# Eleven-block layer stack on one core: scan side work redistributed over VectorE, ScalarE and GpSimd, with new issue orders

## The reference

```python
xc = conv_general_dilated(xi, conv_w, ...)       # 4 taps, depthwise, along time
xi = silu(xc + conv_b)
dt, Bm, Cm = split(xi @ x_proj.T, ...)
dt = softplus(dt @ dt_w.T + dt_b)
dA = exp(dt[..., None] * A);  dBx = (dt * xi)[..., None] * Bm
h  = dA * h + dBx                                 # the recurrence over 512 tokens
y  = sum_over_states(h * C) + xi * D
y  = (y * silu(z)) @ out_proj.T
```

## Time and profile before

| | us |
|---|---|
| median of 3 runs | 3326.03 (3322.09 to 3331.97) |
| profiled execution: its own time | 3321.42 |
| profiled execution: span, first to last instruction | 3319.6 |
| busy PE / DVE / ACT / POOL | 2674.8 / 2515.0 / 1659.4 / 1577.2 |

### The profile page before, as it was taken

How to read it: one execution, slowest core, us unless ns; L and a number is a source line. 1 busy time by engine, 2 the same in 40 slices (tenths; PEclk the granted TensorE clock), 3 DMA queues, 4 the chain that set the end, 5 groups by cost and what they waited for, 6 DMA issues and landing times.

```text
span 3319.6 us, 30398 instructions
## 1 busy us (share of the span) xinstructions
PE 2674.8 (81%) x8498; PEld 889.4 (27%) x8498; DVE 2515.0 (76%) x3637; ACT 1659.4 (50%) x2752; POOL 1577.2 (48%) x1301
## 2 busy tenths in 40 slices
PE   5676757979698988998689976997579877998887
PEld 1222212323122322233222321232122322232222
DVE  1588988787988889788977798878988887246351
...
GB/s 82 55 102 83 96 107 44 78 101 68 93 46 82 76 126 51 90 68 99 109 40 97 69 119 52 72 80 95 106 53 103 77 118 17 45 53 80 43 31 42
DMA packets 160088, 253.13 MB, mean 76 GB/s; under 512 B 20144, under 2 KB 57904, under 8 KB 159664
## 3 DMA queue, kind: packets, MB, share of 16 engines
...
## 4 chain that ended last, share of the span: by engine, by line
PE 50%; DVE 28%; ACT 10%; issue 8%; POOL 3%; DMA 1%; DVEq 0%; SPq 0%; POOLq 0%; ACTq 0%
PE ps L507 50%; DVE rh L1257 7%; DVE nmx L1179 5%; DVE xib L1243 2%; DVE rh L1263 2%; ACT ps L1557 2%; ACT tN L1503 1%; ACT L1304 1%; DVE xif L1243 1%; DVE tF L1121 1%; POOL tF L1632 1%; POOL rb L1612 1%; DVE tF L1126 1%; DVE tL L1168 1%; ACT ps L1317 1%
## 5 line engine op out<-in xcount | busy, mean ns | idle before, releaser
L1257 DVE TENSOR_TENSOR_SCAN rh<-ps,rb 128x512 f32<-128x512 f32 x512 | 622.9, 1217 | 117.0 <-ACT ps L1557 103.4
L1179 DVE TENSOR_REDUCE nmx<-ps 128x1 f32<-128x512 f32 (+3 forms) x864 | 529.9, 661 | 84.9 <-PE ps L507 82.9
L1503 ACT ACTIVATE tN<-ps 128x512 f32<-128x512 f32 (+1 forms) x896 | 460.9, 564 | 230.4 <-PE ps L507 228.2
L1602 POOL TENSOR_TENSOR rh<-rh,cs 128x512 f32<-128x512 f32 x208 | 308.6, 1487 | 437.4 <-DVE rh L1257 437.1
L507 PE MATMUL ps<-tN,strip 128*64 128x512 f32 (+3 forms) x2048 | 484.4, 564 | 12.0 <-DVE hN L1201 9.2
L1612 POOL TENSOR_TENSOR rb<-duf,bs 128x512 f32<-128x512 f32 x256 | 369.1, 1456 | 227.2 <-DVE rh L1257 225.9
L507 PE MATMUL ps<-hF,W 128*128 128x512 f32 x592 | 361.7, 696 | 59.8 <-DVE tF L1121 37.5
L1612 POOL TENSOR_TENSOR rb<-dub,bs 128x512 f32<-128x512 f32 x256 | 369.0, 1459 | 65.9 <-DVE rh L1257 63.1
L507 PE MATMUL ps<-Ks,Qs 48*128 48x512 bf16 (+3 forms) x1024 | 325.8, 409 | 83.8 <-DVE nmx L1179 82.1
L1626 POOL TENSOR_TENSOR tF<-tF,cr 128x512 f32<-128x512 f32 x128 | 172.0, 1345 | 363.8 <-DVE tF L1126 253.0
L507 PE MATMUL ps<-tF,W 128*128 128x512 f32 x544 | 306.7, 656 | 39.7 <-POOL tF L1632 30.9
...
## 6 DMA issues: line engine op xcount, KB each, us to landing
cr<-shares SPq DMA_DIRECT2D x256, 256.0 KB, 3.3
bs<-rowsf SPq DMA_DIRECT2D x128, 256.0 KB, 3.6
cs<-rowsf SPq DMA_DIRECT2D x128, 256.0 KB, 3.2
bs<-rowsb SPq DMA_DIRECT2D x128, 256.0 KB, 3.6
cs<-rowsb SPq DMA_DIRECT2D x128, 256.0 KB, 3.4
...
```

What stands on the lines that cost most here:

```text
L1179: red(nmx[:, 4 * qt + 2 * (i // 4) + a, i % 4:i % 4 + k], o[:, 0:k * nk].rearrange("p (k c) -> p k c", k=k), AX.X, ALU.max, negate=True).t ...
L1257: eng.tensor_tensor_scan(rh[n % NH][:, g, :], PS, rb[n % NBB][:, g, :], 0.0, ALU.mult, ALU.add).then_inc(s_h, 1)
L1503: act(tN[m % NP][:, a, 0:nq], PA[a][:, 0:nq], ACT.Exp).then_inc(s_ex, 1)
L1602: tt(h, h, cs[n % NB][:, :], ALU.mult).then_inc(s_cp, 1)
```

## The change

- The first tap and its bias (32 instructions of 128×512) go from DVE to ACT, as an Identity activation with scale and bias. The wait for the scaled weights of batch 0 goes with it.
- The positive parts (32) go from DVE to ACT, as Relu with a bias. They now stand between |v| and its exp on ACT.
- The products with D (32) go from DVE to ACT, as Copy with a scale, behind the wait for POOL's dt·xi. What waited for DVE's `yi1` now waits for ACT's.
- In the 208 later steps DVE multiplies by C in every fourth step, in place of every second: 52 DVE products of 128×1024 go, and 104 POOL products of 128×512 come.
- DVE's scaling of the weights for M (`setup_later`) is now a step of its own in DVE's list.
- Every string of `ORDER` is new. ACT's list has 138 table loads by the built program, where the list before has 150 (one of these stands ahead of the first activation).

```diff
@@ ORDER: all strings are replaced, as this line of "sp" @@
-        "M1S21M1S43M1S29F1S2F5S1M1F1S5F1S1F1S13P2S2P2S2P1S3P1S6M1S7X1S12F6S4F2S2F1S6M1S4P5F1P1F3S4F3S2F2X1S2F4S2F1S2F4S"
+        "M1S19M1S45M1S32F5M1F1S3F1S2F1S2F1S12P1S2P3S2P1S2P1S7M1S7X1S18F1S1F3S1F1S2F2S2F1S1F1M1S9P5F1P1F3S6F3S2F2X1S2F4S"
...
@@ KINDS @@
-    "pre": chain("in0 in1 xp dt0 dt1", "si0 si1 pj ab0 ex0 ln0 ab1 ex1 ln1",
-                 "c00 c10 c20 c30 xs0 c01 c11 c21 c31 xs1 mx0 dt0 mx1 dt1 yi0 yi1", "du", ln={}),
+    "pre": chain("in0 in1 xp dt0 dt1", "c00 si0 c01 si1 pj ab0 mx0 ex0 ln0 ab1 mx1 ex1 ln1 yi0 yi1",
+                 "c10 c20 c30 xs0 c11 c21 c31 xs1 dt0 dt1", "du", ln={}),
@@ who multiplies by C @@
-            return n < EARLY or n % 2 == 1
+            return n < EARLY or n % 4 == 1
@@ vector_engine, pre @@
-                if j.b == 0:
-                    eng.wait_ge(s_set, SET["mw"])
...
-                    eng.wait_ge(*j.pe(f"in{g}"))
-                    ts(c, PM, cw[:, 4 * g + 3:4 * g + 4], w(f"m{p}_cb", g, g + 1), ALU.mult, ALU.add).then_inc(
-                        *M.by_dve(j, f"c0{g}"))
-                    yield
...
-                        eng.wait_ge(*j.dve(f"c{d - 1}{g}"))
+                        eng.wait_ge(*(j.dve(f"c{d - 1}{g}") if d > 1 else j.act(f"c0{g}")))
...
-                    eng.wait_ge(*j.act(f"ab{g}"))
-                    ts(dt[p][:, g, :], PM, w(f"m{p}_db", g, g + 1), 0.0, ALU.add, ALU.max).then_inc(
-                        *M.by_dve(j, f"mx{g}"))
-                    yield
                     eng.wait_ge(*j.act(f"ln{g}"))
-                    eng.wait_ge(*j.dve(f"mx{g}"))
                     tt(dt[p][:, g, :], dt[p][:, g, :], PM, ALU.add).then_inc(*M.by_dve(j, f"dt{g}"))
-                    yield
-                eng.wait_ge(*j.pool("du"))
-                for g in range(2):
-                    ts(xi[p][:, g, :], xi[p][:, g, :], w(f"m{p}_dd", g, g + 1), None, ALU.mult).then_inc(
-                        *M.by_dve(j, f"yi{g}"))
@@ scalar_engine, pre @@
+                    if (j.b, g) == (0, 0):
+                        eng.wait_ge(s_set, SET["mw"])
+                    eng.wait_ge(*j.pe(f"in{g}"))
+                    act(du[p][:, g, :], PM, ACT.Identity, bias=w(f"m{p}_cb", g, g + 1),
+                        scale=w(f"m{p}_cw", 4 * g + 3, 4 * g + 4)).then_inc(*M.by_act(j, f"c0{g}"))
+                    yield
...
+                    act(dt[p][:, g, :], PM, ACT.Relu, bias=w(f"m{p}_db", g, g + 1)).then_inc(*M.by_act(j, f"mx{g}"))
+                    yield
...
-                    eng.wait_ge(*j.dve(f"mx{g}"))
+                    eng.wait_ge(*j.act(f"mx{g}"))
                     act(PM, a, ACT.Ln, bias=one).then_inc(*M.by_act(j, f"ln{g}"))
+                    yield
+                eng.wait_ge(*j.pool("du"))
+                for g in range(2):
+                    act(xi[p][:, g, :], xi[p][:, g, :], ACT.Copy, scale=w(f"m{p}_dd", g, g + 1)).then_inc(
+                        *M.by_act(j, f"yi{g}"))
                     yield
```

More of the change, by code:

```diff
@@ L61 @@
+        "S2P2S2P2S4F9S2X1S4F4S2F1S1F4S9P4S2P1S2P1S4F1S2F3M1S2F1S2F1S4F3S1F1S3X1S6F4S2F2S2F1S2F1M1S2F1S10P5F1P1F3S5F3S1F"
+        "2X1F1S2F3S2F5S10P2S2P2S2P1S2F1P1F3S2F1S3M1S1F1S2F3S3F1S5F5X1F1S2F1S2F2S6M1S8P4S4F4P1F1P1F1S2F3S2X1F4S2F5S12P4S"
+        "4P1S2P1S2F1S2F3S3F6X1F9P4F6P2F7X1F5P1F1P1F3P2F5P1F1P1F9X1F9P6X1F20"
     ),
     "pe": (
[L63 to L64 removed]
@@ new lines @@
+        "1M1F2S1F1M1F2M1F9L8M1L1X2L1X4L1X3L1X2L2X1L2M1X1L1M1X1L1M2X4M1X2M1X3L1X2L1X4M1L1X5L1X3L1X5M1X2L1X1M1L1A1L2M1A1M"
+        "1A1M1L1A4F1A2F1A2M1A1F2A5F1A5F1A3F2A4F2A19F3A1F4M1F9M1F2M1F6M1F3L1F1L1F1M1L1F2L1M1L1F1L1F2L1F1M1F2L1F1L1F1X2L1"
+        "X14F2X3L1F2X3L1F1X2F2X3L1X1F1X2F2X1F1X2L1F2X3F1X2F2X3F2X3F1L1F1X1L1F1A1M1F1A4M1A2F1A2F1A2M1A4F1A1F1A1F1A2F2A1F"
+        "1A2F1A1F1A2L1M1L1A1L1A2L1A3L1A2L1A2L1A10L1A3L1A1M1X2L1M1L1X3L1X2M1X4L1X4L1X4M1X3L1X7M1X7M1X3L1M1X5M1X1L1X1L1X8"
+        "F1X3F1X3M1X2F2X2F1X1F1L1F1A1F1A4F2A32F1A2F2A2M1F1A2F2A3F1A2F2A1F1A2F2A2F1A2F2A2F1A2F2A2F1A2F2A1M1F1M1F2A2M1F3L"
@@ new lines @@
+        "1F1M1L1F1L2F1L1F2L1F2L1F1M1F2L1F1X2F1X2L1X2M1X1L1X8F2X3F2X3L1F1X3F2X3F1X1L1F2X3F1X2F2X3L1F1X3L1F2X3F2X2F1L1F1X"
+        "1L1F1M1A1F1M1A6F1A2F1A2M1A6F1A1F1A2F1A1F2A2F1A2M1F2L1F1L1A2L1A2F1L1A2L1A2L1A2F1A2M1A2M1A9L1F2L1M1L1A1L1F1X2L1M"
+        "1X1F1M1X2L1X2F1X4M1F2M1F2M1F1X3L1X2L1X6F1X3F1X3M1X2L1F2X4F1X2F1X3L1F1X3F1X4F2X2L2F1X3F2X3F1X2F2X1F1X3F2X1F1X3L"
+        "1F3X1F3A1F2A2F1A2F2A2F1A2F2A2F2A2M1F1A2L1A2F1L1A2F1A4M1A2M1A8L1A2L1A2L1A2F2A8L1A4L1A2M1A4L1A4L1A2X1A1X4A1F1X2L"
+        "1F2X3L1F1X3F3X3L1F2X3F1X1M1X1F2X3L1X1F1X2F2X3F1X2F2X2F1X3L1F2X3F1X2F2X2F2L1F1X1L1F1A1F1A6M1A2F1A8F1A2F1A6F4A1F"
@@ new lines @@
+        "1A1F1A2F2A2L1A2F1L1A2F1L1A2L1A2F1L1A2L1A2L1A4M1A1L2M2F1X2F1M1X1M1X2M1F1M1F1X1A1X1F1X1M1X5F2X4M1F1X1F1M1F1X11M1"
+        "X3L1X2M1X1L1M1X3L1X5F1X3F1X3M1X1L1F2X3L1X1F1X2F1X2F1X3F1L1X3F3L1F2X1L2F3A1F1L1F2A2F1A2M1F2A4F1A2F2A2F1A2F2A2M1"
+        "F1A2M1F2A2F1A2F2A2F2A3F1A3L1A2F1L1M1F1A1L1A1L1A2L1A2F2A12L1A4L1A6L1A2M1X1A1X2L1X2A1F1X2F2X3L1F1X3F2X3F1X2F2X3F"
+        "1X2F2X3F1X1F2X1L1F1X3L1F2X3F1X2F2L1X3F1X1L1F4X3L1X1F2X1L1F1A2F1A7M1A4F1A2F1A4M1A1F1A2F1A1F2A2M1F3M1F1L1F1L1A2F"
+        "1M1L1A2L1A2F1L1A2L1A2L1A8L1A4L1A1X2M1X2F2M1X2M1A1X2F1M1X3L1X2F1L2X3M1F2X2F1M1F1X3F1X1F1X2L1X2L1X8M1X3L1X7M1X4M"
@@ L167 @@
+        "1S4F1S2M1S1F2S1F1S1F3L1S4M1S5L1S1A1S5A1S1A1S6F2S1A1S1F1S2F1A1S4F1S3F1A1S2F1S2F1S13A2S5M1S1F2S1L1F1S3F5S1A1S4A1"
+        "F3A1F3S1F2S4A1S7A1S5A1S3A1S1M1S1A1S12F1S9F3S1F1S1F1M1S2F2S3M1S7F1S1F1S3F1S2F1S3F1A1S3F1S2A1F1S1F1S3A1S5A1S9A1S"
+        "3A1S5A1S2F2A1S1F6S2M1S2A1S1F3S1F3S1F2A2S6A1S10A1S3A1S4A1S4A1S5M1S14F1S2F2S1F1S1F2S1F1S1F1M1F3A1F2A1F2A1F1A4F3A"
+        "1F13A4F3A1F1A1F4A2F8A1F3A1F5A7F1A1F5A1F2A3F8"
     ),
@@ L399, in build @@
         for b in range(B):
-            pre_f, pre_b = ([jm[b, n].pool("du"), jm[b, n].dve("yi1"), (s_rows[p], 16 * (b + 1))] for n, p in
+            pre_f, pre_b = ([jm[b, n].pool("du"), jm[b, n].act("yi1"), (s_rows[p], 16 * (b + 1))] for n, p in
                             (("mf", "f"), ("mb", "b")))
```

191 lines of the change are left out of this document (85 added, 106 removed).

## The result

| | before | after |
|---|---|---|
| median, us (4 runs each on the same chip) | 3326.2 | 3297.2 (3295.98 to 3302.93) |
| ratio, with 95% interval | 1 | 0.9915 (0.9896 to 0.9934) |
| profiled execution: own time / span, us | 3321.42 / 3319.6 | 3298.37 / 3296.5 |

The kernel became faster by 0.85%, some 28 us. The forecast was 3260, a change of −62 us on the profiled execution; the sign was right and less than half of the size came. 3297 lies in the range of 3190 to 3335 and next to the time of rival C (3300).

A forecast was written before the change was run, and what follows sets the result against it. DVE was taken to lead the first two busy stages, close to PE in the middle, PE the tail. From 3321.4: −94 + 10 + 15 + 7 = −62, so 3259, 3264 as median, stated as 3260 us; 8-in-10 range 3190 to 3335.

The forecast's parts named there:

- rival C: PE takes over at once: only DVE's chain share, 58 us, counts against 32 us of costs; −26, 3300; chance 0.20.
- The order, priced at 0 ± 25: All engines' rewoven lists: the same strands overlap in the same way, so 0 us, ±25.
- The weight of 0.6: DVE: 0.6 of the 157 us that leave it counts as gain, 94 us, with bounds 58 and 157.
- its lower bound: DVE's relief counted only by its share of the chain, 28 of 76 points, 37%: 58 us gained.
- the count of 20-us windows: Middle stage: 116 windows sorted by DVE's busy time, counting in full, half or not; 0.55, taken as 0.6.
- The costs of 32 us: On POOL, SBUF and ACT: 10 for the queue, 15 for shared reading, 7 for later exponentials.
- The queue: On POOL: late products delay the next `rb`, then scans and DVE's adds; 10 us, bounds 0 and 57.
- the 7 forecast: On ACT: new work delays exponentials that DVE's scans wait for; 7 us, bounds 0 and 25.
- Shared reading: DVE's adds slowed by POOL's SBUF work: 15 us, bounds 0 and 110; mean add 1.5 to 1.6 us.
- Rival D's point, 1.88: Mean DVE add, in us, from which moved products blocking adds would decide; the rival has +33, 3359; chance 0.15.
- The tail "as long as now": Tail, 560 us, would keep its length; 20 us or more longer would be the order.
- The sign of the queue: DVE waiting for POOL's products or `rb` by more than 30 us in all would show the queue.

The follow-up runs named there:

- short_both_old: old_both with all moved work on POOL and ACT cut to 8 of 512 columns, those values left out; 0.9898 of the kernel before, 3292.58 us.
- old_both: Kernel before with its old lists and both moves (products by C to POOL, three kinds of operations to ACT); 1.0104, 3367.11 us.
- new_order: Kernel before with all strings of `ORDER` new and neither move; 1.0208, 3401.03 us.
- relief_old: Kernel before with the work taken from DVE cut to 8 of 512 columns (from batch 1 on), nothing put elsewhere; 0.9896, 3298.25 us.
- old_tail: Kernel after with the lists of before from a little behind the last scan on; 0.9872 of the kernel before, 3292.79 us.
- relief_two: relief_old plus the 256 expert up-projection matmuls on PE at 256 of 512 columns, those values left out; 0.9771 of the kernel before, 3254.30 us.

## Why the prediction was wrong in size

The table can be walked in two ways from before to after. In the old lists first: relief −34 us (short_both_old), price of the moved work +69 (old_both against it), new lists −63 (after against old_both: 1.0104 − 0.9915). Or in the new lists: the lists alone +69 (new_order), relief −108 (1.0208 − 0.9883), price +11. Both give −28. The prediction had −94, +32 and 0, in all −62.

- **The order, priced at 0 ± 25, is the step that failed by either walk**: −63 or +69, by what it is put on, and more than twice the bound. The prediction treated it as a remainder, since the same strands overlap in the same way; no row had priced it. The table shows that the worth of the moves and that of the lists can't be priced apart.
- **The weight of 0.6 failed in the lists from which it was read.** The 157 us that leave DVE were about right (155.8 by the rows; DVE's busy time fell by 102.5). That 0.6 of them, 94 us, would be gained was not: in the old lists all of them bring 34 us, and the first 97 bring 35, 0.36 each. The prediction had the right number for that beside it, 0.37 from the earlier trace rows, as its lower bound, and set it aside for the count of 20-us windows. A window in which DVE is busy 95% says that DVE is full there. It doesn't say that the other engines can run earlier by what it sheds; in relief_old the waits for exponentials (103.4 to 127.5 us) and PE's share of the chain (50 to 54) grew. In the new lists the weight was 0.66 to 0.71, so by that walk 0.6 was near. That is luck: no row of those lists was read for it.
- **The costs of 32 us were less than half of the price in the old lists** (69: POOL 48, ACT 21) and three times that in the new (11). The queue was looked for behind `rb`, while in old_both PE's wait for the expert products grew, 30.9 to 43.0 us; the prediction named these products and put no price on them. The wait for `rb` did go up in the middle stage, from 12.0 us to 25.5, for a queue priced at 10. But new_order has 28.5 us in all with no product moved, so it is in the main the lists' and not the products'. The wait for exponentials grew by 20 us in the stage for the 7 forecast. Part of that is no cost of the work on ACT: it grew by 24 us in relief_old, where ACT got nothing.
- **Shared reading** came as forecast in size: the mean add is 1.61 us (334.9 over 208), at the upper edge of 1.5 to 1.6, and the adds cost 21 us more in all for 15. Rival D's point, 1.88, was not reached. But new_order has 1.582 without a moved product, and old_both 1.600 in the old lists: lists and products each bring most of the rise alone, and the forecast had only the products. And the adds were not all that is held up: small SBUF work on DVE took more too, and so DVE's busy time is 2412.5 where 2373 was forecast.
- **The sum was helped by luck.** By the first walk it came within 37 us of the time only because two errors to one side (the gain too high by 60, the costs too low by 37) met an order better by 63; the rest is in rounding (its sum gives 3264, and it says 3260). By the second, the gain too low by 14 and the costs too high by 21 met an order worse by 69.
- **The tail "as long as now"** failed by 20 us. The sign was named ahead (20 us or more would be the order), and old_tail shows that it was.
- **Rival C** has the time, 3300, but not the mechanism. Of the 58 us that it grants the relief, the old lists paid 34; its costs of 32 were a middle between the two sets of lists; it had no term for the order either. Its sign, PE's waits for DVE unchanged, did not show (461 to 410 us), and relief_two shows that PE and DVE are both paid.
- **Right**: 100 products with 141.3 us (140); POOL 1721.6 (1735); ACT 1694.2 (1710). **Missed** beside what is named above: the middle stage is 31 us shorter and not 55 to 70; DVE's wait for exponentials in it is 107 us for 94. The sign of the queue, more than 30 us of waiting for `rb` in all, showed with 32.5; by new_order it was a sign of the lists.

What stays open: which places in the new lists make room for POOL's products. The table shows that they do, and PE's wait for `tF` (43.0 in old_both, 13.9 after) points to the expert products in POOL's list. Single places were not tried, so that is a reading and not shown. Open too is how much of the −63 us comes by way of TensorE's clock: the six runs of old_both have 0.818 to 0.827, the four of after 0.836 to 0.840. And since the lists for moved work in the opposite version were made by a simple rule, a better hand could have made old_both, or new_order, faster than they are here.
